# Pacing of the attention's edge gathers: from one count per expert unit, raised by VectorE, to one per quarter unit, raised by ScalarE

## The reference, cut to what matters

```
h = (x @ W_gat)                         # per node: 4 heads x 4 experts, with a_src per head
row[src]                                # for every edge, in the order of its target: a_src and h, 20 numbers
for ei in range(4):                     # experts, on every node
    hh = gelu(x @ W1[ei] + b1[ei])      # 256 -> 512
    y[ei] = hh @ W2[ei] + b2[ei]        # 512 -> 256
```

## Time and profile before

| What | us |
|---|---|
| Median of 3 runs | 3788.47 (3782.95 to 3798.07) |
| The profiled execution | 3779.81 |
| its span, first to last instruction | 3777.8 |
| GpSimd busy in the span | 1704.2 (45%) |
| TensorE matmul busy | 2708.7 (72%) |
| ScalarE busy | 692.7 (18%) |
| VectorE busy | 1621.8 (43%) |

### The profile page before, as it was taken

One profiled execution on the slowest core, in us unless ns is written; L12 is line 12 of the kernel. 1 busy time (PEld: TensorE's weight loads), 2 busy tenths in 40 slices (PEclk: granted clock), 3 DMA queues, 4 the chain that ended last, 5 costly groups with the idle time before them and its releaser, 6 DMA issues. The chain is left out here.

```text
span 3777.8 us, 34904 instructions
## 1 busy us (share of the span) xinstructions
PE 2708.7 (72%) x10528; PEld 1927.9 (51%) x10528; DVE 1621.8 (43%) x3135; ACT 692.7 (18%) x1082; POOL 1704.2 (45%) x1746
## 2 busy tenths in 40 slices
PE   3887888788788777799998865766766766765007
PEld 2666666666666655666665542433434433434006
DVE  6444555455454467666778960000000000001784
ACT  1111111111111123223332220111101101101005
POOL 1565656556565510022221216666666666662211
PEclk8777777777777779999999986878878877877558
DMA  7433333333333332200000013222222212213415
GB/s 259 131 105 91 106 101 106 99 100 104 97 108 93 99 99 74 68 23 23 23 23 12 9 12 70 37 36 37 37 36 37 37 31 37 41 30 109 145 59 229
DMA packets 215309, 280.82 MB, mean 74 GB/s; under 512 B 95634, under 2 KB 166312, under 8 KB 213706
## 3 DMA queue, kind: packets, MB, share of 16 engines
q0 software_dynamic: 68416, 133.35, 14.6%
q1 hardware_dynamic: 105994, 108.62, 9.3%
q10 hardware_dynamic: 40832, 38.01, 3.2%
HBM read 215.36 MB, written 64.48 MB: 74 GB/s over the span
## 5 line engine op out<-in xcount | busy, mean ns | idle before, releaser
L421 POOL DMA_INDIRECT xg<-xn_dram,gidx x784 | 743.9, 949 | 526.2 <-DVE gidx L562 283.2
L1962 POOL DMA_INDIRECT er<-row_dram,gi x784 | 739.9, 944 | 430.7 <-issue 411.9
L2023 PE MATMUL ps_en<-ew,hid 128*128 128x256 f32 x1568 | 404.5, 404 | 216.6 <-issue 213.4
L2095 DVE TENSOR_TENSOR eo<-ps_en,eb_r 128x1024 f32<-128x1024 f32 (+1 forms) x52 | 60.5, 1163 | 1157.7 <-remote 851.5
L2013 PE MATMUL ps_em<-zT_all,ew 128*128 (+2 forms) x832 | 420.4, 646 | 190.9 <-issue 123.7
L456 PE MATMUL ps_e<-we,eaT 65*128 65x256 f32 x1568 | 507.2, 480 | 69.3 <-issue 56.2
L473 PE MATMUL ps_a<-arena 128*128 128x256 f32 x1568 | 522.1, 491 | 34.6 <-ACT arena L506 26.4
L2023 PEld LDWEIGHTS ps_en<-ew,hid 128*128 128x128 f32 x1568 | 314.7, 202 | 311.6 <-issue 271.6
L473 PEld LDWEIGHTS ps_a<-arena 128*128 128x128 f32 x1568 | 399.0, 256 | 134.2 <-ACT arena L506 34.8
L456 PEld LDWEIGHTS ps_e<-we,eaT 65*128 65x128 f32 x1568 | 356.8, 239 | 138.8 <-issue 74.0
L2013 PEld LDWEIGHTS ps_em<-zT_all,ew 128*128 128x128 f32 x832 | 172.9, 215 | 419.6 <-issue 386.8
(11 more groups left out here) (291 smaller groups left out, 2877.0 us busy)
## 6 DMA issues: line engine op xcount, KB each, us to landing
eaT<-in_eaT SPq DMA_DIRECT2D x98, 256.0 KB
eo_dram<-eo ACTq DMA_DIRECT2D x48, 512.0 KB
eo<-eo_dram SPq DMA_DIRECT2D x12, 2048.0 KB
xg<-xn_dram,gidx POOLq DMA_INDIRECT x784
er<-row_dram,gi POOLq DMA_INDIRECT x784
xm<-xm_dram SPq DMA_DIRECT2D x24, 512.0 KB
erow<-arena ACTq DMA_DIRECT2D x1, 10240.0 KB
erow<-er SPq DMA_DIRECT2D x196, 40.0 KB
```

Source lines behind the costliest of these rows:

```text
L421: pool.indirect_dma_start(xg[:, q, b, :], None, M["xn_dram"], bass.IndirectOffsetOnAxis(ap=gidx[:, q, b:b + 1], axis=0)).then_inc(s_g[q][b ...
L1962: pool.indirect_dma_start(er[:, r, b, :], None, M["row_dram"], bass.IndirectOffsetOnAxis(ap=gi[:, r, b:b + 1], axis=0)).then_inc(s_get[r], 16)
L2023: m = pe.matmul(ps_n[b][:, t, :], hid[:, b, c, t * P:(t + 1) * P], w2[:, e, c, :], start=(c == 0), stop=(c == KE - 1))
```

## The change

The count s_pace is raised at another place, by another engine, in finer steps, and POOL waits for it at each four:

- POOL's wait ahead of a batch (for j + 1) becomes a wait ahead of each four (for 4j + r + 1), with its marker increment of s_go.
- ScalarE raises s_pace by one behind each of the four activations of a rise, 208 times in all, by AHEAD at its start and by 256 at its end.
- VectorE no longer touches s_pace.
- AHEAD goes from 4 (batches, which is 16 fours) to 8 (fours, which is two batches).

The last batch stays unpaced. Gathers, stores, lists, matmuls, activations and their other waits stay as they are.

```diff
-        AHEAD = 4
+        AHEAD = 8
...
                 with pool.Fori(0, last) as j:
 
-                    pool.wait_ge(s_pace, j + 1)
-                    pool.sem_inc(s_go, 1)
                     for r in range(R):
+                        pool.wait_ge(s_pace, j * R + (r + 1))
+                        pool.sem_inc(s_go, 1)
                         gather(j, r)
                 for r in range(R):
                     gather(last, r)
...
                         nc.scalar.activation(hid[:, b, c, 0:w], ps_m[c][:, 0:w], ACT.Gelu,
                                              bias=b1[:, e * KE + c:e * KE + c + 1]).then_inc(s_ge, 1)
+                        act.sem_inc(s_pace, 1)
...
                 act.sem_inc(s_st[0], 16)
                 act.sem_inc(s_st[1], 16)
+                act.sem_inc(s_pace, AHEAD)
...
                     store(u, e, e % 2, NG, 1)
+                act.sem_inc(s_pace, E2 // (P * MB))
...
                     nc.vector.tensor_tensor(eo[:, b, 0:T, :], ps_n[b][:, 0:T, :], b2[:, e, None, :].broadcast_to([P, T, D]), ALU.add).then_inc(s_e, 1)
-                    dve.sem_inc(s_pace, 1)
 
                 dve.sem_inc(s_e, 2)
-                dve.sem_inc(s_pace, AHEAD)
...
                     give(u, e, e % 2, u // 2, 1)
-                dve.sem_inc(s_pace, E2 // (R * P * MB))
```

## The result

The changed kernel takes 3844.5 us (median of four runs, 3832.2 to 3851.9), the kernel before 3791.6 on the same chip (3783.0 to 3798.1): a ratio of 1.0138, interval 1.010 to 1.0176. It is slower, by 53 us.

A forecast was written before the change was run, and what follows sets the result against it. No compute engine fills the stage; GpSimd's gathers (979 us), pauses (174) and tail (51.5) make it up. Pauses +50, expert ends +10 and lead -2 give +58 on 3779.8: 3838 us, range 3745 to 3890, likeliest case 3808 to 3875.

The forecast's parts named there:

- Where a pause ends: GpSimd's pauses ended by a give: count now comes with the next rise's first activation, each ending 2.2 us later.
- How many pauses: Gather pauses: runs merge to 32, each with a long pause, 236 us against 186: +50 us, ends -29 and +120.
- Expert ends: Three places where both stores precede the next rise, so counts wait one more second layer: +10 us, ends 0 and 21.
- The lead: GpSimd's allowed lead: halved in fours, not shorter in time; last gather some 2 us later, tail shorter: -2 us.
- Instructions: ScalarE's 208 increments, GpSimd's 144 more waits, VectorE's 52 fewer increments: 0 us; upper end 43 us for the waits.
- no change: Second rival, about 3788 us: merging offsets later pause ends, or pacing doesn't reach the crawl's cause; chance 0.23.
- third: Faster rival, 3749 us: dry GpSimd gets fours singly with pauses between, TensorE doesn't crawl; chance 0.22.
- fourth: Much slower rival, 3908 us: every run ends at 16 gathers, next rise blocked behind a late give; chance 0.12.

The follow-up runs named there:

- The kernel with the 144 waits: Kernel before with GpSimd waiting ahead of each four, VectorE still raising the count, by four at each give, start value 16: 3798.8 us, ratio 1.0002.

## Why the prediction was right

The forecast was +58 us on the profiled execution, 3838; that execution grew by 52.4, and the median is 3844.5. The prediction's +1.3% sets a sum on the profiled execution beside the median of the runs, which is 8.7 us higher; like with like its +58 us are +1.5%. Measured are +1.4%, by the median and by the profiled execution.

The mechanism was right. That the sum came so close is in part luck: for the gathers it had +50 and +10, together +60, and 52.7 were measured; for the tail it had -2, and +5.1 were measured. Two misses of 7 us cancel, and the stage's earlier start took another 5.1 off. By its steps:

- *Where a pause ends*: right, and the term that decides. Predicted +2.2 us behind the give with the 1.18 us to the gather kept; measured 2.25 and 1.16. The long pauses were to be 9.5 and are 9.0, the short ones were to be 6.3 and are 6.4. The kernels with delays of 0, 1.2, 2.2 and 3.4 us show that it is the cause.
- *How many pauses*: the 236 us forecast and the 239 measured aren't the same thing. The 236 left out the expert ends, which had a term of their own; the 239 hold 17 us of them. Without these it is 222, or +36 and not +50. The picture was only half right, too. Runs of 16 fell from 14 to 8, as merging wants; runs of 32 didn't rise, 12 before and 11 now, and runs of 20 to 28 and single fours took their place. The pattern nearest to the forecast, 18 runs of 32, came where GpSimd waited once for a batch, with the same sum, 240. The fine wait changes where runs break and not what the pauses cost.
- *Expert ends*: +10, range 0 to 21. Two of three places pay, 8.9 and 8.0 us over the ordinary long pause, together 17. The term was 7 us too small, and inside its bounds. At the first expert end the trace shows why nothing is paid:

```profile
2577.03 0.94 POOL L1962 DMA_INDIRECT er<-row_dram,gi  x1 [4.79 <-ACTq L2062]
...
2580.47 1.22 DVE L2098 TENSOR_TENSOR eo<-ps_en,eb_r 128x1024 f32<-128x1024 f32 x1 [5.38 <-PE ps_en L2023]
...
2599.98 1.23 DVE L2098 TENSOR_TENSOR eo<-ps_en,eb_r 128x1024 f32<-128x1024 f32 x1 [18.29 <-remote]
```

  A run of gathers starts at 2577.03, and the first of the two gives runs 3.4 us into it, ahead of the crawl. Only the second is left for the pause, which is an ordinary short one of 6.2 us (the gather at 2602.89).
- *The lead*: the argument that it isn't shorter in time stands; with a start value of 16 nothing is regained. The -2 for the tail was wrong in sign: the tail grew by 5.1. A later count doesn't simply shift the last gather against the experts; what sets the tail wasn't tried by itself.
- *Instructions*: 0 expected. The kernel with the 144 waits shows +0.02%, within 0.3% either way; ScalarE's increments weren't tried without a delay. The upper end of 43 us, 1.1%, is excluded; the 146 us named for ScalarE's increments would be more than the whole loss.

Of the rivals, *no change* needed merging to pay for the later ends: a merged run did have the long pause, as was held against it. In its other form the crawl hung on something that the pacing doesn't reach. Against that stand the kernels whose GpSimd issues no gather for 2 to 3 us behind each 8: the other engines' loops branch as often as before, and TensorE runs at clock 0.99 to 1.00. The Trainium skill's Runtime: NRT & Kernel Launch, section Instruction fetch mechanics, has an engine wait for a fetch behind a taken branch out of the resident window; the traces don't bear this out as the cause of the crawl. The 7 packets of the earlier trace rows had spoken against it, too. The *third*, single fours, did come, for 213 us: from 2651 to 2864 activations come one at a time and open single fours. But it brought nothing. The changed kernel has 418 TensorE records and 145 gathers there, the kernel before 419 and 148 in the same stretch:

```profile
2651.00:2864.00 213.00, 146.61 (x418) 87.61 (x417) 11.02 (x9) 23.93 (x37) 136.16 (x145) 0.79 0.22 38
```

The fours of that rival were to come with TensorE at full speed; here they came inside the crawl, with runs of 20 and 24 among them. The regime that it describes exists: short runs with pauses over 2 us give full speed. It takes a fixed spacing of GpSimd's own to get there; the experts' counts don't, for they come four at once where a crawl ends, and singly and late within one. The *fourth*, all runs of 16, had the wrong direction: they became fewer.

## What to carry to other kernels

Ask of a throttle's signal when it comes and not how fine it is: a count placed behind two more instructions of another engine's stream costs its delay at the pauses, here 53 us of 3792 for a delay of 2.2 us, and four counts raised in a burst are no finer than one. Where a wait exists to keep one engine from disturbing others, look for the shortest pause that stops the disturbance, and let the disturbing engine take it by itself, at a fixed spacing: here 2.2 us behind each 8 gathers (ratio 0.9828) beat a feedback through two engines that let each disturbance run its full course. And stop it as soon as the disturbed work is done, but look at the helpers of what goes on: here, without any pause, the engine that fetches the lists fell behind. A fixed spacing, and a fixed batch at which it stops, are tuned to one input; the feedback isn't.

## What the runs showed of the hardware

- *Indirect gathers from GpSimd in an unbroken run* (one per 1.249 us) slow SyncE, and TensorE, which shares no data with them: SyncE's DMA issues from 0.34 to 0.70 us, TensorE from some 3.4 records per us (2053 in 600) to 1.0 (625 in 600), at clock 1.00 and 0.62. For TensorE it sets in at some 18 to 20 us into a run, and it ends 2.9 to 5.8 us behind the last gather. Runs of 8 with 2.2 us between them show none of it (2052 records), with 1.8 us some (1601), runs of 16 with 3.0 us a good deal (1120). What the engines share there wasn't found out; the pauses needn't be idle, and the gathers needn't have landed.
- *An increment behind an activation in ScalarE's stream doesn't wait for its end.* The activations at 2426.40 are four in 2.42 us; the profile has ScalarE's first increment at 2426.4 as well, for 17 ns, though an activation takes 662 ns. GpSimd's gather came 1.16 us behind, as soon as behind the start of a give whose increment follows it on VectorE (1.18), though the give itself takes 1.23 us. A count raised in this way tells that an instruction has started, not that its result is there.
- *What pacing is worth*: without it the kernel takes 4081 us (one run), 8% more, though its 1117 us of gathers are the shortest of all versions.
